# First row block of the attention scores as one full-precision product, another order of the turned sets

## Chip, cores and metric

One core of one Trainium2 chip. The time is that of one launch in device microseconds (us). The profile shows TensorE in two columns, PE (matmul) and PEld (weight load), beside DVE (VectorE), ACT (ScalarE), POOL (GpSimd) and SP (SyncE, which issues the DMAs).

## The reference, cut to what matters

Sixteen sequences of 512 tokens, width 128, 16 heads of 64: a modulated layer norm, causal attention, and a mixture of 8 experts with top 2. The change touches the attention alone.

```python
h = _layernorm(x) * (1 + ca) + sa
q, k, v = einsum('bsd,dhk->bshk', h, W_Q), ... W_K, ... W_V
scores = einsum('bqhc,bshc->bhqs', q, k) / sqrt(64)
probs = softmax(where(triu(ones, k=1), -1e6, scores))
z = einsum('bhqs,bshc->bqhc', probs, v)
x = x + ga * (einsum('bqhc,chd->bqd', z, W_out) + b_out)
h = _layernorm(x) * (1 + cb) + sb
x = x + gb * moe(h)
```

## The kernel before

First the attention of all 16 sequences (some 1150 us), then the experts of all. In the attention the unit of work is a pair of heads: `b` is the sequence, `p` the pair (8 in each, 128 in all), and `body` of TensorE runs once for each pair. Products that need more than the rounded fp32r format are made of three: high by high, low by high, high by low, where the low part is what rounding left (`split_product`, and the loop at L570 to L579 for scores). ScalarE rounds the high part (`round_q`, `round_k`), VectorE subtracts for the low part (`rest_q`, `rest_k`).

The causal score matrix of one head has four row blocks of 128 queries: row r has (r + 1) x 128 keys. `UNITS` groups them: unit 0 is row 3 (PSUM banks 2 and 3, one for each head), unit 1 is rows 2 and 0 (banks 4 and 5), unit 2 is row 1 (banks 6 and 7). The two heads lie in the two halves of the partitions, so a score product takes 64 rows of the array.

In order, TensorE's iteration for pair p (L716 to L793): scores of p, units 0, 1, 2; the product of probabilities and values for pair p-2 (`weigh_values`, full fp32, one half of the array's columns for each head); projections q and k of pair p+1; for some p one or more value chunks (`V_CHUNKS`), for p = 2 and 6 a part of the output projection; then the transposes of the probabilities of p-1 in three sets. Set 0 is 8 blocks of head 0, set 1 is 8 blocks of head 1, set 2 is 4 blocks of both. A block is turned in two halves (16, 16 and 8 transposes). Their order before is 2, 0, 1: set 2 to banks 4 and 5, set 0 to banks 6 and 7, set 1 to banks 0 and 1 (`T_PAIR`).

The other engines, for each pair: VectorE masks the scores and takes the row maxima (`mask_and_max`, L1239; in the order of units, head 0 then head 1), computes `rest_z`, `rest_q`, `rest_k`, and copies sets 2 and 0 out of PSUM (`evac_T`, L1232, 512 and 1024 elements for each partition), each after its transposes are counted in `t_ps`. ScalarE computes the exponentials with their sums (`exponentials`, L954), rounds z, q and k, copies a value chunk, and copies set 1 (`evac_T`, L945). GpSimd multiplies the eight row parts by the inverse sums (L501), as VectorE's `invert_sums` (L1248) has given them; it counts them in `p_norm`.

Banks tie the engines together. Scores of unit 1 go where VectorE's first copy of the iteration before has read, those of unit 2 where its second copy has: L569 waits for `t_dve` at 2(8b+p) - 3 and - 2, two counts a pair.

```python
if not young and u > 0:
    pe.wait_ge(t_dve, pair(2, b, p) - (3, 2)[u - 1])
```

The transposes wait for the masks that read their banks (`s_masked`) and for all eight norms of their pair (`p_norm`). `batches_from_middle` only places the loop's seam; each engine's order is the one written.

Of the kernel before, what the change touches and what calls it, by code (L numbers as in the profile page):

```python
# [20 lines left out]
UNITS = [[3], [2, 0], [1]]  # L21
ROW_AT = {3: 0, 2: 512, 0: 896, 1: 1024}
ROW_IN_BANK = {3: 0, 2: 0, 0: 384, 1: 0}
# [21 lines left out]
def masked_at(h, u):  # L45

    return (h, 2 + 2 * h, 6 + h)[u]
# [10 lines left out]
def adaln_moe_kernel(nc, resid, W_Q, W_K, W_V, W_out, b_out, W1, b1, W2, b2, Wr, br, c_in, wmod, out):  # L58
# [10 lines left out]
    with ExitStack() as ctx:  # L69
# [13 lines left out]
        T_PAIR, T_PAIR_END = [6, 0, 4], [0, 4, 6]  # L83
        T_PLACE = [2, 3, 1]
# [68 lines left out]
        side = banks[:, 4:6, 256:512].rearrange("p a (t s) -> p t a s", s=DH)  # L153
# [45 lines left out]
        with ExitStack() as pb:  # L199
# [31 lines left out]
            rdenom = sa("rdenom", [P, 2, 8])  # L231

# [123 lines left out]
            q_lo = sem("q_lo")  # L356
            k_lo = sem("k_lo")
# [15 lines left out]
            with nc.Block() as block:  # L373
# [67 lines left out]
                def _(pool):  # L441
# [47 lines left out]
                    def body(b, first, last):  # L489
                        for p in range(NP):  # L490
# [6 lines left out]
                            for h in range(2):  # L497
                                for r in ROW_ORDER:
# [4 lines left out]
                                        .then_inc(p_norm, 1)  # L503

                    batches(pool, body)
# [14 lines left out]
                def _(pe):  # L520
# [38 lines left out]
                    def scores(b, p, u, begin, young):  # L559
# [4 lines left out]
                        if young and not begin:  # L564

                            pe.wait_ge(s_masked, (2, 6, 8)[u])
# [3 lines left out]
                        for r in UNITS[u]:  # L570
                            n = (r + 1) * P
# [37 lines left out]
                    def values(b, p, n, i):  # L609
# [5 lines left out]
                        pe.wait_ge(s_masked, pair(8, b, p) + (7, 2)[n])  # L615
# [100 lines left out]
                    def body(b, first, last):  # L716
                        for p in range(NP):
# [14 lines left out]
                            scores(b, p, 0, begin, young)  # L732
                            if p == 5 and last:
                                pe.wait_ge(x_mid, b)
                            if p == 6 and last:
                                pe.wait_ge(r_full, 1)
                            scores(b, p, 1, begin, young)
# [34 lines left out]
                            if not begin:  # L772
                                pe.wait_ge(s_masked, done + 6)
# [6 lines left out]
                                if 0 in put:  # L780
                                    pe.wait_ge(v_done, 8 * b + now[len(put) - 1 - put[::-1].index(0)] + 1)
                                if p == 6 and not last:
                                    pe.wait_ge(h_full, b + 2)
                                    if not first:
                                        pe.wait_ge(x_mid, b)
                                wait_alone(pe, s_masked, done + 8)
                                transposes(*prev, 0, T_PAIR[0])
# [58 lines left out]
                    wait_alone(pe, p_norm, pair(8, end, NP))  # L846
                    transposes(end, NP - 1, 2, T_PAIR_END[2])
                    wait_alone(pe, hid, 2)
# [71 lines left out]
                def _(act):  # L920
# [187 lines left out]
                    def rear(b, p, first, last):  # L1108
# [16 lines left out]
                        if begin:  # L1125
                            round_weights(3)
# [466 lines left out]
```

## Time and profile before

| | us |
|---|---|
| runs of the kernel before, median of 3 (lowest, highest) | 1879.13 (1876.46, 1879.55) |
| the profiled execution, its own time | 1881.74 |
| its span, first to last instruction | 1879.9 |
| PE busy in it | 1865.9 |
| DVE / ACT / POOL busy | 1642.9 / 1558.2 / 729.7 |
| mean granted TensorE clock | 0.998 |

Busy time overlaps between engines. A matmul's duration in the profile holds its way through the array, so that consecutive ones overlap: what one costs is the distance from its start to the next one's start. "x2" in a row of the timeline is a group of two instructions; here mostly the two heads, which start together.

### The profile page before, as it was taken

What the parts mean: (1) busy time and instruction counts of PE and PEld (TensorE: products, weight loads), DVE (VectorE), ACT (ScalarE), POOL (GpSimd) and SP (SyncE); (2) the same over time, 40 slices, a digit from 0 to 9 for tenths busy, and PEclk for the clock granted to TensorE, in tenths of its full rate; (3) what the DMA queues carried; (4) which work ended last, traced back from release to release, by engine and by line L of the source; (5) the groups of instructions that cost most, each with busy time, mean ns of one, the idle gap of its engine ahead of it and who ended that gap; (6) DMA issues with size and microseconds to landing.
All of it is one profiled execution on the core that took longest, in us unless ns stands there. A gap on an engine that the chain in (4) does not pass through costs nothing.

```text
span 1879.9 us, 50582 instructions
## 1 busy us (share of the span) xinstructions
PE 1865.9 (99%) x15334; PEld 1431.6 (76%) x15334; DVE 1642.9 (87%) x4388; ACT 1558.2 (83%) x3664; POOL 729.7 (39%) x1212
## 2 busy tenths in 40 slices
PE   8999999999999999999999999999999999999999
PEld 6777777777777777777777777888888888888887
DVE  7898888888888888888888888989998999999998
ACT  6988988988998998998988988777777777777775
POOL 3454454454454444544445442222222222222221
PEclk9999999999999999999999999999999999999999
DMA  4200000000000000000000003111111111111111
GB/s 122 69 2 1 1 1 1 1 1 1 1 1 0 1 1 0 1 1 0 1 1 1 1 2 91 52 51 51 51 51 51 51 51 51 51 51 51 51 56 51
DMA packets 42622, 50.04 MB, mean 27 GB/s; under 512 B 3160, under 2 KB 24464, under 8 KB 42512
## 3 DMA queue, kind: packets, MB, share of 16 engines
q1 hardware_dynamic: 42256, 48.41, 8.1%
q0 software_dynamic: 256, 0.53, 0.1%
q14 instruction: 86, 0.70, 0.1%
q8 instruction: 24, 0.39, 0.1%
HBM read 44.47 MB, written 4.46 MB: 26 GB/s over the span
## 4 chain that ended last, share of the span: by engine, by line
PE 97%; DVE 1%; ACT 1%; issue 1%; DMA 0%; SPq 0%; ACTq 0%; DVEq 0%
PE banks L605 16%; PE banks L578 13%; PE banks L592 9%; PE banks L684 6%; PE banks L686 6%; PE banks L685 6%; PE banks L703 6%; PE banks L705 6%; PE banks L704 6%; PE banks L523 6%; PE banks L525 5%; PE banks L524 5%; PE banks L627 2%; PE banks L629 2%; PE banks L628 2%
## 5 line engine op out<-in xcount | busy, mean ns | idle before, releaser
L501 POOL TENSOR_SCALAR probs<-probs,rdenom 128x512 f32<-128x512 f32 (+3 forms) x1024 | 523.9, 533 | 584.5 <-DVE rdenom L1248 584.5
L954 ACT ACTIVATE probs<-probs,neg_max 128x512 f32<-128x512 f32 (+3 forms) x1024 | 561.8, 551 | 52.0 <-DVE neg_max L1239 52.0
L1059 ACT ACTIVATE hidden<-banks,b_cols 128x512 f32<-128x512 f32 x512 | 349.5, 688 | 177.7 <-PE banks L686 177.4
L1418 DVE TENSOR_TENSOR hid_lo<-hidden,hid_hi 128x512 fp32r<-128x512 f32 x512 | 380.3, 754 | 56.8 <-ACT hid_hi L1067 42.0
L1239 DVE CUSTOM_DVE_ANT_0 probs<-banks,mask_w 128x512 f32<-128x512 f32 (+3 forms) x1024 | 427.1, 482 | 0.7 <-PE banks L578 0.7
L487 POOL TENSOR_TENSOR acc<-acc,y_w 128x512 f32<-128x512 f32 x110 | 151.4, 1377 | 462.8 <-DVE y_w L1431 461.0
L605 PE MATMUL banks<-probs_T,v_sb 128*64 128x512 f32 (+3 forms) x2048 | 304.6, 440 | 0.3 <-issue 0.3
L1232 DVE COPY probs_T<-banks 128x512 f32<-128x512 f32 (+1 forms) x256 | 232.6, 949 | 30.0 <-PE banks L592 30.0
L605 PEld LDWEIGHTS banks<-probs_T,v_sb 128*64 128x64 f32 x2048 | 136.4, 137 | 155.7 <-issue 119.4
L592 PEld LDWEIGHTS banks<-ident,probs 64*128 64x128 f32 x5120 | 171.7, 140 | 45.3 <-issue 45.3
L684 PE MATMUL banks<-h_hi,w_hi 128*128 128x512 f32 x512 | 205.8, 402 | 0.1
L685 PE MATMUL banks<-h_hi,w_lo 128*128 128x512 f32 x512 | 199.6, 390 | 0.0
L686 PE MATMUL banks<-h_lo,w_hi 128*128 128x512 f32 x512 | 199.6, 390 | 0.0
L703 PE MATMUL banks<-hid_hi,w_hi 128*128 128x512 f32 x508 | 197.8, 389 | 0.0
L705 PE MATMUL banks<-hid_lo,w_hi 128*128 128x512 f32 x508 | 197.7, 389 | 0.0
L704 PE MATMUL banks<-hid_hi,w_lo 128*128 128x512 f32 x508 | 197.6, 389 | 0.0
L954 ACT ACTIVATION_READ_ACCUMULATOR probs<-probs,neg_max 128x1 f32 x1024 | 192.7, 188 | 0.0
L592 PE MATMUL banks<-ident,probs 64*128 64x64 f32 x5120 | 189.1, 226 | 0.7 <-ACT hidden L1059 0.6
L578 PE MATMUL banks<-k_hi,q_hi 64*128 64x512 f32 (+3 forms) x1024 | 177.6, 340 | 4.2 <-DVE probs_T L1232 2.1
L1252 DVE TENSOR_TENSOR z_lo<-banks,z_hi 128x512 fp32r<-128x512 f32 x128 | 88.3, 690 | 94.2 <-ACT z_hi L966 94.2
L578 PE MATMUL banks<-k_hi,q_lo 64*128 64x512 f32 (+3 forms) x1024 | 167.3, 320 | 0.0
L578 PE MATMUL banks<-k_lo,q_hi 64*128 64x512 f32 (+3 forms) x1024 | 166.5, 319 | 0.0
(182 smaller groups left out, 3393.3 us busy)
## 6 DMA issues: line engine op xcount, KB each, us to landing
w_rows<-w_kept SPq DMA_DIRECT2D x128, 256.0 KB, 4.5
x_all<-in_L_attn_resid_dram SPq DMA_DIRECT2D x16, 256.0 KB, 2.8
w_raw<-in_L_ffn_W_dram SPq DMA_DIRECT2D x16, 256.0 KB, 4.8
out_dram<-y_result SPq DMA_DIRECT2D x15, 256.0 KB, 2.3
v_sb<-in_L_attn_W_V_dram SPq DMA_DIRECT2D x1, 512.0 KB, 9.8
hidden<-in_L_attn_W_out_dram POOLq DMA_DIRECT2D x2, 256.0 KB, 7.7
v_sb<-in_L_attn_W_Q_dram SPq DMA_DIRECT2D x1, 448.0 KB, 6.3
v_sb<-in_L_attn_W_K_dram SPq DMA_DIRECT2D x1, 448.0 KB, 7.5
```

The costliest lines, as they stand in the source:

```text
L501: pool.tensor_scalar(part, part, rdenom[:, p % 2, 4 * h + r:4 * h + r + 1], 1.0, ALU.mult, ALU.mult)\
L578: mm = pe.matmul(S_BANK[u][h][:, at:at + n], q[own, p % 2, rows], k[own, p % 2, 0:n], start=start, stop=stop)
L592: mm = pe.transpose(banks[:, first_bank + half, at:at + DH], probs[own, p % 2, h, src:src + P], ident[own, own])
L605: mm = pe.matmul(bank[h * DH:(h + 1) * DH, c * P:S], v_sb[:, c, hc:hc + DH], probs_T[:, h, KEY_AT[c]:KEY_AT[c] + n], start=(c == 0), stop= ...
L684: pe.matmul(banks[:, c, :], w1_hi[:, e, cols], h_hi[:, :], start=True, stop=False)
L685: pe.matmul(banks[:, c, :], w1_lo[:, e, cols], h_hi[:, :], start=False, stop=False)
L686: pe.matmul(banks[:, c, :], w1_hi[:, e, cols], h_lo[:, :], start=False, stop=True)\
L703: pe.matmul(y_bank, w2_hi[:, e, c, :], hi, start=(c == 0), stop=False)
L954: act.activation(part, part, ACT.Exp, bias=neg_max[:, p % 2, col:col + 1], scale=-1.0, accum_out=denom[:, p % 2, col:col + 1]).then_inc(p_ ...
L1059: act.activation(hidden[:, e % 2, c, :], banks[:, c, :], ACT.Gelu, bias=b1_cols[:, e * HC + c:e * HC + c + 1]).then_inc(hid, 1)
L1239: dve.tensor_tensor_reduce(out=probs[:, p % 2, h, at:at + n], in0=S_BANK[u][h][:, col:col + n], in1=mask_w[:, 512 - n:512], scale=-SCALE, ...
L1418: dve.tensor_tensor(hid_lo[:, e % 2, c, :], full, hi.bitcast(F32), ALU.subtract)\
```

## The change

The row blocks are grouped anew: unit 1 is row 2 alone, unit 2 is rows 1 and 0 (banks 6 and 7). Row 0 (128 x 128) is no longer three fp32r products for each head, but one in full fp32, from `q_full` and `k_full`, the sums of high and low parts. GpSimd makes these sums in a new step `join`, two instructions a pair behind the norms, and TensorE waits for them (`q_whole`, `k_whole`) ahead of row 0.

The sets are turned in the order 0, 2, 1: set 0 to banks 4 and 5, set 2 to banks 6 and 7, set 1 to banks 0 and 1 as before. Set 0 waits for four norms and the masks of units 0 and 1, set 2 for all. The waits for value chunk, h and x that go with banks 6 and 7 come ahead of set 2. VectorE's copies follow: set 0 first, then set 2. `invert_sums` moves behind the two masks of unit 0. On ScalarE both value chunks stand ahead of the exponentials of head 0, unit 2, and the copy of set 1 stands ahead of the exponentials of head 1, unit 2.

```diff
 ROW_ORDER = [3, 2, 0, 1]
-UNITS = [[3], [2, 0], [1]]
+UNITS = [[3], [2], [1, 0]]
 ROW_AT = {3: 0, 2: 512, 0: 896, 1: 1024}
-ROW_IN_BANK = {3: 0, 2: 0, 0: 384, 1: 0}
+ROW_IN_BANK = {3: 0, 2: 0, 0: 256, 1: 0}
 HEAD_COLS = 1280
...
-    return (h, 2 + 2 * h, 6 + h)[u]
+    return (h, 2 + h, 4 + 2 * h)[u]
...
-        T_PAIR, T_PAIR_END = [6, 0, 4], [0, 4, 6]
-        T_PLACE = [2, 3, 1]
+        T_PAIR, T_PAIR_END = [4, 0, 6], [6, 4, 0]
+        T_PLACE = [1, 3, 2]
...
-        side = banks[:, 4:6, 256:512].rearrange("p a (t s) -> p t a s", s=DH)
+        side = banks[:, 6:8, 256:512].rearrange("p a (t s) -> p t a s", s=DH)
...
             rdenom = sa("rdenom", [P, 2, 8])
+            q_full = sa("q_full", [P, 2, P])
+            k_full = sa("k_full", [P, 2, P])
...
             q_lo = sem("q_lo")
+            q_whole, k_whole = sem("q_whole"), sem("k_whole")
             k_lo = sem("k_lo")
             t_dve = sem("t_dve")
             s_masked = sem("s_masked")
...
+                            if not (last and p >= NP - 2):
+                                join(*after(*after(b, p)))
...
+                    def join(b, p):
...
+                        wait_alone(pool, q_lo, pair(1, b, p) + 1)
+                        pool.tensor_tensor(q_full[:, p % 2, :], q_hi2[:, p % 2, 0:P].bitcast(F32),
+                                           q_lo2[:, p % 2, 0:P].bitcast(F32), ALU.add).then_inc(q_whole, 1)
+                        wait_alone(pool, k_lo, pair(1, b, p) + 1)
+                        pool.tensor_tensor(k_full[:, p % 2, :], k_hi2[:, p % 2, 0:P].bitcast(F32),
+                                           k_lo2[:, p % 2, 0:P].bitcast(F32), ALU.add).then_inc(k_whole, 1)
...
+                    join(0, 0)
+                    join(0, 1)
                     batches(pool, body)
...
-                            pe.wait_ge(s_masked, (2, 6, 8)[u])
+                            pe.wait_ge(s_masked, (2, 4, 8)[u])
                         if not young and u > 0:
...
                         for r in UNITS[u]:
+                            if r == 0:
+                                pe.wait_ge(q_whole, pair(1, b, p) + 1)
+                                pe.wait_ge(k_whole, pair(1, b, p) + 1)
+                                at = ROW_IN_BANK[0]
+                                for h in range(2):
+                                    own = slice(h * DH, (h + 1) * DH)
+                                    mm = pe.matmul(S_BANK[u][h][:, at:at + P], q_full[own, p % 2, :],
+                                                   k_full[own, p % 2, :], start=True, stop=True)
+                                continue
                             n = (r + 1) * P
                             at = ROW_IN_BANK[r]
                             rows = slice(r * P, (r + 1) * P)
...
-                        pe.wait_ge(s_masked, pair(8, b, p) + (7, 2)[n])
+                        pe.wait_ge(s_masked, pair(8, b, p) + (6, 2)[n])
                         toks, cols = slice(t * P, (t + 1) * P), slice(half * 512, half * 512 + 512)
                         split_product(V_BANK[n], (h_hi[:, toks], h_lo[:, toks]),
                                       (wv[0][:, cols], wv[1][:, cols])).then_inc(v_ps, 1)
...
                             scores(b, p, 0, begin, young)
+                            scores(b, p, 1, begin, young)
                             if p == 5 and last:
                                 pe.wait_ge(x_mid, b)
                             if p == 6 and last:
                                 pe.wait_ge(r_full, 1)
-                            scores(b, p, 1, begin, young)
                             if begin:
                                 pe.wait_ge(b_ok, 1)
                             scores(b, p, 2, begin, young)
...
                             if not begin:
-                                pe.wait_ge(s_masked, done + 6)
+                                pe.wait_ge(s_masked, done + 4)
+                                wait_alone(pe, p_norm, pair(8, *prev) + 4)
+                                transposes(*prev, 0, T_PAIR[0])
+                                if 0 in put:
+                                    pe.wait_ge(v_done, 8 * b + now[len(put) - 1 - put[::-1].index(0)] + 1)
+                                if p == 6 and not last:
+                                    pe.wait_ge(h_full, b + 2)
+                                    if not first:
+                                        pe.wait_ge(x_mid, b)
+                                pe.wait_ge(s_masked, done + 8)
                                 if p == 4 and last:
                                     attention_T_beside(b - 1)
                                 if p == 5 and last:
                                     norm_T_beside(0)
                                 wait_alone(pe, p_norm, pair(8, *prev) + 8)
                                 transposes(*prev, 2, T_PAIR[2])
-                                if 0 in put:
-                                    pe.wait_ge(v_done, 8 * b + now[len(put) - 1 - put[::-1].index(0)] + 1)
-                                if p == 6 and not last:
-                                    pe.wait_ge(h_full, b + 2)
-                                    if not first:
-                                        pe.wait_ge(x_mid, b)
-                                wait_alone(pe, s_masked, done + 8)
-                                transposes(*prev, 0, T_PAIR[0])
                                 if not young:
                                     pe.wait_ge(z_done, pair(1, *prev))
                                 if has_next:
...
                     wait_alone(pe, p_norm, pair(8, end, NP))
+                    transposes(end, NP - 1, 0, T_PAIR_END[0])
+                    wait_alone(pe, hid, 2)
                     transposes(end, NP - 1, 2, T_PAIR_END[2])
-                    wait_alone(pe, hid, 2)
-                    transposes(end, NP - 1, 0, T_PAIR_END[0])
                     wait_alone(pe, z_done, pair(1, end, NP - 1))
                     transposes(end, NP - 1, 1, T_PAIR_END[1])
                     pe.wait_ge(o_half, B)
...
                         exponentials(b, p, 0, 1)
-                        exponentials(b, p, 1, 1, [2])
+                        exponentials(b, p, 1, 1)
                         if not (first and p < 2):
                             round_z(*two_before(b, p))
                         if has_next and not begin:
...
                         put = chunk_banks(p, first, last)
-                        if now:
-                            values_out(b, put[0], now[0])
-                        exponentials(b, p, 1, 1, [0])
-                        if len(now) > 1:
-                            values_out(b, put[1], now[1])
+                        for bank, i in zip(put[:2], now[:2]):
+                            values_out(b, bank, i)
                         exponentials(b, p, 0, 2)
...
                             values_out(b, n, i)
-                        exponentials(b, p, 1, 2)
+                        if begin:
+                            exponentials(b, p, 1, 2)
                         if p == 5 and last:
-                            act.wait_ge(t_dve, pair(2, *prev) + 1)
+                            act.wait_ge(t_dve, pair(2, *prev) + 2)
                             router_h_evac(0, in_halves(hf[:, :]), side)
                         if p == 6 and not last:
                             half_out(b)
...
                             evac_T(*prev, first and p == 1)
+                            exponentials(b, p, 1, 2)
                         if begin:
                             round_weights(3)
...
                         begin, nxt = first and p == 0, after(b, p)
+                        mask_and_max(b, p, 0, 0)
+                        mask_and_max(b, p, 1, 0)
                         if not begin:
                             invert_sums(*before(b, p))
-                        mask_and_max(b, p, 0, 0)
-                        mask_and_max(b, p, 1, 0)
                         mask_and_max(b, p, 0, 1)
                         if begin:
                             rest_q(*nxt)
...
                         if not begin:
+                            evac_T(*prev, 0, first and p == 1, T_PAIR[0])
                             evac_T(*prev, 2, first and p == 1, T_PAIR[2])
                         if p == 4 and last:
                             add_attention(b - 1)
-                        if not begin:
-                            evac_T(*prev, 0, first and p == 1, T_PAIR[0])
...
                     split_expert(1, 3)
+                    evac_T(end, NP - 1, 0, False, T_PAIR_END[0])
                     evac_T(end, NP - 1, 2, False, T_PAIR_END[2])
-                    evac_T(end, NP - 1, 0, False, T_PAIR_END[0])
                     weights(0)
                     for e in range(4, E):
                         split_expert(1, e)
...
```

## Rows read from the trace of the kernel before

**Rows 1.** The page: busy time of each engine, and the chain that ended last.

```profile
PE 1865.9 (99%) x15334; PEld 1431.6 (76%) x15334; DVE 1642.9 (87%) x4388; ACT 1558.2 (83%) x3664; POOL 729.7 (39%) x1212
...
PE 97%; DVE 1%; ACT 1%; issue 1%; DMA 0%; SPq 0%; ACTq 0%; DVEq 0%
```

**Rows 2.** Timeline, PE, two iterations' transposes; start us, us, engine, line, operation.

```profile
407.61 1.48 PE L592 MATMUL banks<-ident,probs 64*128 64x64 f32 x40
...
415.57 1.47 PE L592 MATMUL banks<-ident,probs 64*128 64x64 f32 x40
```

**Rows 3.** Timeline, PE, the scores of the pair between them.

```profile
408.90 0.48 PE L578 MATMUL banks<-k_hi,q_hi 64*128 64x512 f32 x2
...
410.21 0.22 PE L578 MATMUL banks<-k_hi,q_hi 64*128 64x128 f32 x2
...
410.38 0.28 PE L578 MATMUL banks<-k_lo,q_hi 64*128 64x128 f32 x2
410.49 0.34 PE L578 MATMUL banks<-k_hi,q_hi 64*128 64x256 f32 x2
...
410.78 0.28 PE L578 MATMUL banks<-k_lo,q_hi 64*128 64x256 f32 x2
410.99 0.65 PE L605 MATMUL banks<-probs_T,v_sb 128*64 128x512 f32 x2
```

**Rows 4.** Timeline, PE, full fp32: first and last key block of one product with values.

```profile
403.04 1.08 PE L605 MATMUL banks<-probs_T,v_sb 128*64 128x512 f32 x4
...
405.02 0.39 PE L605 MATMUL banks<-probs_T,v_sb 128*64 128x128 f32 x4
```

**Rows 5.** Timeline, DVE, its copies beside the transposes at 407.61.

```profile
407.67 0.69 DVE L1225 TENSOR_TENSOR k_lo<-banks,k_hi 128x512 fp32r<-128x512 f32 x1
408.27 1.81 DVE L1232 COPY probs_T<-banks 128x512 f32<-128x512 f32 x2
410.00 0.19 DVE L1248 RECIPROCAL rdenom<-denom 128x8 f32<-128x8 f32 x1
```

**Rows 6.** Timeline, PE and DVE, a copy that waited for its transposes.

```profile
189.69 0.79 PE L592 MATMUL banks<-ident,probs 64*128 64x64 f32 x18
...
190.20 0.69 DVE L1232 COPY probs_T<-banks 128x512 f32<-128x512 f32 x1 [0.23 <-PE banks L592]
```

**Rows 7.** Timeline, DVE and PE, scores of row 1 that waited for a copy.

```profile
1108.80 1.21 DVE L1232 COPY probs_T<-banks 128x1024 f32<-128x1024 f32 x1
1109.93 0.19 DVE L1248 RECIPROCAL rdenom<-denom 128x8 f32<-128x8 f32 x1
...
1110.07 0.39 PE L578 MATMUL banks<-k_hi,q_hi 64*128 64x256 f32 x2
1110.29 0.28 PE L578 MATMUL banks<-k_hi,q_lo 64*128 64x256 f32 x2
...
1110.62 0.65 PE L605 MATMUL banks<-probs_T,v_sb 128*64 128x512 f32 x2
```

**Rows 8.** Timeline, DVE and PE, the iteration with p = 2.

```profile
181.05 1.47 PE L592 MATMUL banks<-ident,probs 64*128 64x64 f32 x40
...
181.28 0.75 DVE L1262 SCALAR_TENSOR_TENSOR attn_T<-banks,gate_cols,o_part 128x512 f32<-128x512 f32 x1 [1.53 <-PE banks L629]
181.95 1.81 DVE L1232 COPY probs_T<-banks 128x512 f32<-128x512 f32 x2
...
184.43 1.94 PE L605 MATMUL banks<-probs_T,v_sb 128*64 128x512 f32 x10
```

**Rows 9.** Timeline, ACT, its copy of set 1 and the exponentials after it.

```profile
409.58 1.00 ACT L945 ACTIVATE probs_T<-banks 128x1024 f32<-128x1024 f32 x1
410.79 0.72 ACT L954 ACTIVATE probs<-probs,neg_max 128x512 f32<-128x512 f32 x1 [0.20 <-DVE neg_max L1239]
```

**Rows 10.** Timeline, POOL: eight norms; and the page's group of its sums of two tensors.

```profile
410.36 4.09 POOL L501 TENSOR_SCALAR probs<-probs,rdenom 128x512 f32<-128x512 f32 x8 [3.98 <-DVE rdenom L1248]
...
L487 POOL TENSOR_TENSOR acc<-acc,y_w 128x512 f32<-128x512 f32 x110 | 151.4, 1377 | 462.8 <-DVE y_w L1431 461.0
```

## The prediction

> **What bounds the kernel now.** The page comes first: PE is busy 1865.9 of 1879.9 us, and the chain that ended last is PE for 97% [rows 1]. So every microsecond taken off TensorE's own stream counts, unless another engine hands its data over later than the shortened stream wants it. How much each hand-over has in reserve isn't in the page. I read it from the timeline of ordinary pairs, where nobody is shown to wait: from the start T of one pair's transposes to the next is 7.96 us [rows 2]. All times below are counted from T = 407.61. Scores begin at T + 1.29, row 0 at T + 2.60, row 1 at T + 2.88, the product with values at T + 3.38 [rows 3]. From there to the next T are 415.57 - 410.99 = 4.58 us that the change leaves as they are. The other half of the iteration belongs to VectorE, whose two copies run from T + 0.66 to T + 2.47 [rows 5]. Unit 1 of the next scores needs the first of them, unit 2 the second.
>
> **What TensorE's stream saves.** Row 0 takes 410.49 - 410.21 = 0.28 us a pair [rows 3], 36 us in 128 pairs. Its later steps are 0.11 us apart though 128 columns pass in half of that (the 256-column steps aren't longer): weight loads set the pace, and they go on setting it in row 1. The new product: one of full fp32 is two instructions for each head. Four of 128 columns span 0.39 us of which 0.28 is the last pair's duration, so the two heads go side by side and a step costs 0.11 us [rows 4]. For row 0 that makes 2 x 0.11 = 0.22. These rows split the array by columns; the scores split it by rows, and no row here shows full fp32 in that form. Bounds: 0.22 (two steps, as there) to 0.44 (four in a row). I take 0.22, because in every split form in the rows (transposes, scores, values) the heads start together as "x2".
> Without any wait: row 1 would start at T + 2.60 (its weights load under row 2), its three steps 0.12 + 0.12 + 0.11, row 0 0.22, then the 0.10 that the switch to the other split costs (410.99 - 410.78 = 0.21, less the 0.11 of a 256-column pass) [rows 3]. That is T + 3.27 for the product with values, 0.11 earlier than now: 14 us in 126 pairs, 0.8%.
>
> **What the new order of copies takes.** Now the 512-element copy of set 2 goes first. It needs only 8 transposes and VectorE is free later than that, so the copies run right behind `rest_k`, at T + 0.66 [rows 5]. In the new order the first copy needs the 16 transposes of set 0. Twenty starts in 1.47 us, the last 0.22 long and the first gap 0.12, give 0.063 us for a pair of transposes [rows 2], so the eighth pair starts at T + 0.49. A copy that waits starts 0.26 to 0.27 us behind its last transposes (190.20 against 189.69 + 0.12 + 2 x 0.063) [rows 6]: T + 0.76. The 1024-element copy hands over after 1.13 us (1109.93 - 1108.80) [rows 7], the 512-element one lasts 0.68 (1.81 less 1.13) [rows 5]. The second copy ends at T + 0.76 + 1.13 + 0.68 = T + 2.57 to 2.58, which is 0.1 later than today. But unit 2 is wanted 0.28 earlier, since row 0 has left the place ahead of it: at T + 2.60, and its weights sooner. Today's reserve of 0.40 us (T + 2.88 against 2.47) shrinks to 0.02.
> What too little reserve costs is seen where scores of row 1 wait: the copy ends at 1110.01, the product is shown at 1110.07 and the next step comes 0.22 later instead of 0.17, and from the first to the product with values it is 0.55 instead of 0.50, as the first weights load in the open [rows 3, 7]. For the new unit 2 this gives 0.055 from the copy, then 0.22 + 0.12 + 0.11 for row 1, 0.22 for row 0 and 0.10 for the switch: T + 2.575 + 0.055 + 0.775 = T + 3.41. Today it is T + 3.38. **The pair gets 0.03 us longer**, though TensorE has 0.11 us less to do. Unit 1's wait (first copy ends at T + 1.97, its first product is wanted at T + 2.07) loses up to 0.08 us, hidden by the later wait of unit 2.
> **The pair after p = 2** is worse. There `gate_attention` holds the copies until T + 0.90 (181.95 against 181.05) in either order. The second ends at 181.95 + 1.13 + 0.68 = 183.76, the product with values starts at 184.59, today at 184.43 [rows 8]: 0.16 us longer, 15 times.
>
> **The other edits**, each with what hides it.
> GpSimd's two sums a pair: a norm of 128 elements is a part of 4.09 us for eight, a sum of two tensors of 512 takes 1.38 us [rows 10], so 0.3 to 1.4 us for each; I take 0.55. The queue holds norms for 4.1 of 7.96 us, and the sums come behind them, ahead of the next norms. Their inputs are ready by T + 0.8 (`rest_k` ends at 408.36 [rows 5]), their reader is row 0 of the next scores, at T + 2.95. Cost 0; at 1.4 each they would be done at T + 3.3 and hold row 0 up by 0.3.
> `invert_sums` behind two masks: VectorE's sum is the same, the norms start 1.2 to 1.3 us later, at T + 4.0 (410.36 - 407.61 + 1.25 [rows 2, 10]) and end at T + 8.1, which is 0.15 into the next transposes. Set 0 asks for half of them and set 2 for all, at 0.55 into the transposes: 0.4 us of reserve. Cost 0.
> ScalarE: the copy of set 1 starts when its transposes are done, T + 1.52 (20 pairs and the 0.26), instead of T + 1.97 [rows 9]; head 1's last two exponentials (some 0.9 us) follow, and the next pair's first one starts at T + 3.3 instead of T + 3.18. It has one exponential fewer ahead of `round_z`, so z, q and k are rounded no later than now, and q and k wait for TensorE anyway. Nobody waits for ScalarE; cost 0. At the end of an iteration ScalarE is free about 0.05 us before set 1 is turned, so nothing is lost in waiting.
> The waits for value chunks, h and x move behind 16 transposes, to a later place; cost 0, gain 0, as PE shows no wait there. Start and end (the first two pairs, the last sets): within 1 us.
>
> **The sum.** 111 pairs x 0.03 + 15 x 0.16 = 3.3 + 2.4 = 5.7 us. The profiled execution gives 1881.74 + 5.7 = 1887.4 us. It lies 2.6 above the median of the runs, 1879.13, so for the median I forecast **1885 us**, 0.3% slower.
>
> **Rivals.**
> *The heads don't go side by side in row 0*, so the change doesn't do what it says. If the instructions started in strict program order (head 0 twice, then head 1 twice) row 0 would take three steps instead of two; behind the wait that is 0.11 us more in 128 pairs, 14 us: 1899 us. Against it: four 512-column instructions with values span 1.08 us, of which 0.6 is the last pair, so four start within two steps [rows 4]. Wholly in a row: 28 us, 1913.
> The Trainium skill ("TensorE: Matmul & The Clock Gate", Part 3, The mechanism) says matmuls are in program order in start and end, "strict FIFO, no reordering". By that rule this rival holds; the rows with values don't agree with it, and none shows the split by rows.
> *The copies don't bind*: if the second copy came 0.1 us sooner than I make it (a sooner start, or weights that load ahead of the wait), the whole 0.11 us would stay: 14 us, 1865 us. For it: my reserve of 0.02 us is the difference of long sums. Against: a copy has never started less than 0.26 behind its transposes in the rows, and half of the gain needs 0.09.
> *The norms come late*: if GpSimd's norms and sums end over 0.4 us later than I reckon, set 2 waits at every pair. At 0.1 us a pair that is 13 us: 1898 us.
>
> **Chances.** Forecast with its own spread (a pair from -0.02 to +0.07 us, 1877 to 1889): 0.60. Heads one after another 0.17, of which 1899 0.13. Copies don't bind 0.13, half of that gain 0.06. Norms late 0.04. Range: 1868 to 1901 us, which leaves out the full gain and the worst of the first rival. A measurement of this kernel can tell 0.2% from no change (1875.4 to 1882.9). Within the forecast most lies above that: slower 0.40, same 0.18, faster 0.02. With the rivals: slower 0.61, same 0.20, faster 0.19.
>
> **What the profile after would show.** Row 0 as four full fp32 instructions, two steps of 0.11 us, where the first rival has three or four. VectorE's copies in the order 1024, 512, each time with a wait of about 0.1 us for transposes ahead of the first. A line in the waits that PEld at the scores waits for VectorE's copy, over a hundred times. A distance from transposes to transposes of 7.98 to 8.00 us in ordinary pairs; 7.85 would prove the second rival. POOL busy some 140 us more. I am wrong if the scores' waits aren't there, or if the ordinary pair is shorter than 7.94.

## The result, and the profile after

The changed kernel takes 1886.5 us (median of 5 runs, 1885.94 to 1887.52), the kernel before beside it 1879.5 us: ratio 1.0038, 95% interval 1.0027 to 1.0050. It is 0.4% slower; 1885 us was forecast. The profiled execution of the changed kernel took 1886.59 us, 4.9 more than that of the kernel before.

From the page after: span, busy time, the chain that ended last.

```profile
span 1884.7 us, 50756 instructions
...
PE 1867.5 (99%) x15078; PEld 1399.2 (74%) x15078; DVE 1660.1 (88%) x4388; ACT 1559.1 (83%) x3664; POOL 847.5 (45%) x1468
...
PE 96%; DVE 1%; ACT 1%; issue 1%; POOL 0%; DMA 0%; SPq 0%; ACTq 0%; DVEq 0%; POOLq 0%
```

The page hardly differs from that of before [rows 1]: 256 matmuls fewer and PE as busy as ever, since a matmul that waits for its weights is drawn as busy (the 384-column one below takes 0.41 us, before it took 0.33). The list of waits (engine and line, who was waited for, us in all, times, longest), before and after, says more:

```profile
PEld banks L578 <- DVE probs_T L1232: 3.9, 5, 1.9
```

```profile
PEld banks L603 <- DVE probs_T L1257: 35.5, 124, 1.6
```

TensorE's weights for scores (L603) now wait for a copy of VectorE (L1257) 124 times; before, such a wait was there 5 times. In an ordinary pair the wait that is listed is that of unit 1, for the first copy. Weight load (PEld) of the 384-column product:

```profile
409.98 0.19 PEld L603 LDWEIGHTS banks<-k_hi,q_hi 64*128 64x128 f32 x2 [0.25 <-DVE probs_T L1257]
```

Timeline of the changed kernel, PE, one ordinary pair (start us, us, engine, line):

```profile
407.94 1.47 PE L617 MATMUL banks<-ident,probs 64*128 64x64 f32 x40
...
410.01 0.41 PE L603 MATMUL banks<-k_hi,q_hi 64*128 64x384 f32 x2
410.26 0.34 PE L603 MATMUL banks<-k_hi,q_lo 64*128 64x384 f32 x2
...
410.61 0.35 PE L603 MATMUL banks<-k_hi,q_hi 64*128 64x256 f32 x2
410.80 0.28 PE L603 MATMUL banks<-k_hi,q_lo 64*128 64x256 f32 x2
...
411.04 0.38 PE L593 MATMUL banks<-k_full,q_full 64*128 64x128 f32 x4
411.35 0.65 PE L630 MATMUL banks<-probs_T,v_sb 128*64 128x512 f32 x2
```

And DVE in the same pair:

```profile
407.98 0.69 DVE L1250 TENSOR_TENSOR k_lo<-banks,k_hi 128x512 fp32r<-128x512 f32 x1
408.70 1.82 DVE L1257 COPY probs_T<-banks 128x1024 f32<-128x1024 f32 x2
```

With T = 407.94 the first copy starts at T + 0.76 and the second ends at T + 2.58 (408.70 + 1.82). Unit 1 starts at T + 2.07, as before, but its first step is 0.25 instead of 0.17. Unit 2 is shown to start at T + 2.67, its first step is 0.19 instead of the 0.12 of a hidden weight load, and the product with values starts at T + 3.41. It was T + 3.38 [rows 3]. Row 0 itself went as hoped: four instructions in 0.38 us, 0.31 from its start to the next product, switch included. After p = 2 the gated attention holds the copies, as before [rows 8]; PE and DVE of the changed kernel:

```profile
391.16 1.48 PE L617 MATMUL banks<-ident,probs 64*128 64x64 f32 x40
...
392.05 1.81 DVE L1257 COPY probs_T<-banks 128x1024 f32<-128x1024 f32 x2
...
394.69 0.65 PE L630 MATMUL banks<-probs_T,v_sb 128*64 128x512 f32 x2
```

That is T + 3.53, forecast 3.54. Seven pairs in a row, from the transposes after p = 2 on, in the kernel before and then in the changed one:

```profile
391.02 1.47 PE L592 MATMUL banks<-ident,probs 64*128 64x64 f32 x40
...
451.00 1.47 PE L592 MATMUL banks<-ident,probs 64*128 64x64 f32 x40
```

```profile
391.16 1.48 PE L617 MATMUL banks<-ident,probs 64*128 64x64 f32 x40
...
451.49 1.47 PE L617 MATMUL banks<-ident,probs 64*128 64x64 f32 x40
```

59.98 us became 60.33: 0.35 more, where the working gave 0.16 + 6 x 0.03 = 0.34. The eighth pair brings it to some 0.39 a sequence, or 6 us in 126 pairs. The two profiled executions differ by a little less. A possible reason is seen in the stretch 0 to 36 us and the stretch 1090 to 1160 us (busy time of each engine, then the granted clock of TensorE), before and after:

```profile
0.00:36.00 36.00, 29.70 (x199) 24.07 (x201) 23.18 (x76) 22.74 (x54) 10.99 (x26) 0.95 0.46 129
1090.00:1160.00 70.00, 67.23 (x651) 48.44 (x650) 58.30 (x156) 57.88 (x140) 25.51 (x48) 0.98 0.18 55
```

```profile
0.00:36.00 36.00, 29.43 (x208) 22.91 (x208) 25.89 (x86) 24.43 (x60) 14.27 (x34) 1.00 0.45 132
1090.00:1160.00 70.00, 65.51 (x641) 46.05 (x638) 58.76 (x167) 57.39 (x146) 35.14 (x67) 1.00 0.11 30
```

The granted clock of the execution before was 0.95 and 0.98 in the mean of these stretches, so it was at the lower of its two levels (1.2 and 2.4 GHz) for a part of them; in the execution after it was 1.00. These are single executions, so I ascribe no microseconds of the median to it.

### The profile page after: what moved, and what is told of

Same layout as the page of the kernel before. It is cut to its first block, busy times and chain, and to the rows that moved or that the text cites. A ratio compares the mean times of both kernels' runs of the same rounds, so it can differ in the third digit from the quotient of the medians.

```text
span 1884.7 us, 50756 instructions
## 1 busy us (share of the span) xinstructions
PE 1867.5 (99%) x15078; PEld 1399.2 (74%) x15078; DVE 1660.1 (88%) x4388; ACT 1559.1 (83%) x3664; POOL 847.5 (45%) x1468
## 4 chain that ended last, share of the span: by engine, by line
PE 96%; DVE 1%; ACT 1%; issue 1%; POOL 0%; DMA 0%; SPq 0%; ACTq 0%; DVEq 0%; POOLq 0%
PE banks L630 15%; PE banks L603 12%; PE banks L617 9%; PE banks L709 6%; PE banks L710 6%; PE banks L711 6%; PE banks L728 6%; PE banks L730 6%; PE banks L729 6%; PE banks L539 6%; PE banks L541 5%; PE banks L540 4%; PE banks L652 2%; PE banks L654 2%; PE banks L653 2%; PE banks L593 1%
## 5 line engine op out<-in xcount | busy, mean ns | idle before, releaser
L1264 DVE CUSTOM_DVE_ANT_0 probs<-banks,mask_w 128x512 f32<-128x512 f32 (+3 forms) x1024 | 433.5, 479 | 0.5 <-PE banks L603 0.4
L1257 DVE COPY probs_T<-banks 128x1024 f32<-128x1024 f32 (+1 forms) x256 | 233.0, 952 | 39.5 <-PE banks L617 38.2
L971 ACT ACTIVATE probs_T<-banks 128x1024 f32<-128x1024 f32 x128 | 131.3, 1026 | 52.7 <-PE banks L617 52.6
L603 PE MATMUL banks<-k_hi,q_hi 64*128 64x512 f32 (+2 forms) x768 | 159.9, 412 | 5.4 <-DVE probs_T L1257 3.2
L1093 ACT ACTIVATE hid_hi<-hidden 128x512 fp32r<-128x512 f32 x256 | 161.1, 629 | 0.0
```

Source lines behind the costliest of these rows:

```text
L603: mm = pe.matmul(S_BANK[u][h][:, at:at + n], q[own, p % 2, rows], k[own, p % 2, 0:n], start=start, stop=stop)
L1264: dve.tensor_tensor_reduce(out=probs[:, p % 2, h, at:at + n], in0=S_BANK[u][h][:, col:col + n], in1=mask_w[:, 512 - n:512], scale=-SCALE, ...
```

## Experiments

All ratios are to the kernel before, run on the same chip; times in a pair are counted from the start of its transposes, T.

### The product alone

```diff
 UNITS = [[3], [2, 0], [1]]
...
                         for r in UNITS[u]:
+                            if r == 0:
+                                pe.wait_ge(q_whole, pair(1, b, p) + 1)
+                                pe.wait_ge(k_whole, pair(1, b, p) + 1)
+                                ...
```

(and `join` on GpSimd, as in the change; nothing else.)

> The kernel before with one part of the change alone: row 0 as one full fp32 product with GpSimd's sums; units, order of the sets, VectorE and ScalarE as before. My theory (the product saves 0.11 us a pair of TensorE's time and VectorE's second copy took it away): unit 2 is wanted at T + 2.82, the second copy ends at T + 2.47, so nothing waits; product with values 0.11 us earlier in each pair, 14 us less, ratio to the kernel before 0.9925. Rival A (the product saves nothing on TensorE, or the sums on GpSimd slow another engine): ratio 1.000 or above. Rival B (three small products cost less than the start distances say): half the gain, 0.996.

Measured: 1867.26 us, ratio 0.9939 (0.9926 to 0.9953). PE and DVE in an ordinary pair:

```profile
410.76 1.47 PE L617 MATMUL banks<-ident,probs 64*128 64x64 f32 x40
...
413.35 0.38 PE L593 MATMUL banks<-k_full,q_full 64*128 64x128 f32 x4
413.49 0.36 PE L603 MATMUL banks<-k_hi,q_hi 64*128 64x256 f32 x2
...
414.02 0.65 PE L630 MATMUL banks<-probs_T,v_sb 128*64 128x512 f32 x2
```

```profile
411.57 1.81 DVE L1257 COPY probs_T<-banks 128x512 f32<-128x512 f32 x2
```

The product with values starts at T + 3.26, 0.12 earlier than before. The second copy ends at T + 2.62 (411.57 + 1.81 - 410.76) and row 1, which needs it, is shown at T + 2.73: the reserve is down to 0.1 us and still enough. The saving in TensorE's time was priced rightly for an ordinary pair, and no cost of the sums shows there. In the run it is a little less: 11 us between the medians (interval 9 to 14), where 14 were expected. The timelines of the two profiled executions do differ by some 0.88 us a sequence, 14 us in 16; why the medians differ by less stays open. This version is faster than the kernel before by 0.6% and, with both ratios to that kernel, than the changed one by 1.0%.

### The second copy made shorter

The changed kernel, where VectorE's copy of set 2 takes head 0's part only; head 1's part of these blocks keeps the first pair's values.

```diff
-                        dve.tensor_copy(*turned(u, first_bank)).then_inc(t_dve, 1)
+                        out, turned_p = turned(u, first_bank)
+                        if u == 2 and not begin:
+                            out, turned_p = out[:, 0], turned_p[:, 0]
+                        dve.tensor_copy(out, turned_p).then_inc(t_dve, 1)
```

> The changed kernel, but VectorE's copy of set 2 takes head 0's half alone (256 elements of 512; head 1's part of these blocks keeps what the first pair left), all else as changed. My theory: the second copy ends 0.27 us sooner, T + 2.30, and no longer holds unit 2; only unit 1's wait for the first copy is left (0 to 0.08 us): product with values at T + 3.27 to 3.33, ratio to the kernel before 0.994 to 0.997. If the wait for the second copy were not what ate the gain, the ratio would stay at 1.004.

Measured: 1877.08 us, ratio 0.9988 (0.9979 to 0.9998). PE and DVE:

```profile
404.51 1.47 PE L617 MATMUL banks<-ident,probs 64*128 64x64 f32 x40
...
406.58 0.42 PE L603 MATMUL banks<-k_hi,q_hi 64*128 64x384 f32 x2
406.83 0.34 PE L603 MATMUL banks<-k_hi,q_lo 64*128 64x384 f32 x2
...
407.18 0.29 PE L603 MATMUL banks<-k_hi,q_hi 64*128 64x256 f32 x2
...
407.86 0.65 PE L630 MATMUL banks<-probs_T,v_sb 128*64 128x512 f32 x2
```

```profile
405.27 1.56 DVE L1260 COPY probs_T<-banks 128x1024 f32<-128x1024 f32 x2
```

The copies end 0.26 us sooner, and unit 2 takes 0.12 for its first step again: its weight load starts 0.18 us ahead of the product (at 407.00), in the changed kernel 0.04 (at 410.57). The product with values starts at T + 3.35 instead of 3.41. But unit 2 still starts at T + 2.67, and the listed wait of the weights is unchanged:

```profile
PEld banks L603 <- DVE probs_T L1260: 35.5, 124, 1.6
```

That wait is unit 1's: its first step is 0.25 instead of 0.17, with the first copy ending at T + 1.98, less than a weight load (0.19) ahead of T + 2.07. So of the 0.15 us between T + 3.26 and T + 3.41 the second copy accounts for 0.06 and the first for the 0.08 or so that are left. The expectation was missed by a little: the ratio lies above the 0.994 to 0.997 (its interval too), and T + 3.35 above the 3.27 to 3.33.

### Row 0 as three products in the changed order

```diff
                         for r in UNITS[u]:
-                            if r == 0:
-                                ...
-                                continue
```

(`join` is left out too.)

> The changed kernel with row 0 as three fp32r products again (as the last of unit 2) and no sums on GpSimd; all orders as in the changed kernel. My theory: behind the wait for the copy each pair has 0.22 + 0.12 + 0.12 + 0.11 + 0.11 + about 0.2 us to the product with values, T + 3.50, 0.12 us more than before in ordinary pairs: 17 us more, ratio 1.009. If the copy's wait did not set the pace it would be 1.000, and if GpSimd's sums were what costs in the changed kernel it would be under 1.004.

Measured: 1893.03 us, ratio 1.0079 (1.0064 to 1.0095). PE:

```profile
409.52 1.47 PE L594 MATMUL banks<-ident,probs 64*128 64x64 f32 x40
...
412.18 0.35 PE L580 MATMUL banks<-k_hi,q_hi 64*128 64x256 f32 x2
...
412.98 0.65 PE L607 MATMUL banks<-probs_T,v_sb 128*64 128x512 f32 x2
```

Unit 2 is shown to start at T + 2.66, as in the changed kernel (2.67), and the product with values at T + 3.46. The start is the same whatever is multiplied behind it. That the second copy sets it isn't shown: it is T + 2.67 with the shorter copy too, since unit 1 comes 0.08 us late. What the full product saves behind the start is 0.05 us in the timeline, not the 0.09 that I had taken, and 6.5 us between the medians. The three small products cost less than I took: in this timeline the first of row 0 is followed by the next after 0.06 us.

### The inverse sums late, alone

```diff
-                        if not begin:
-                            invert_sums(*before(b, p))
                         mask_and_max(b, p, 0, 0)
                         mask_and_max(b, p, 1, 0)
+                        if not begin:
+                            invert_sums(*before(b, p))
```

> The kernel before with the inverse sums moved behind the two masks of unit 0, nothing else. My theory: the norms end at T + 8.1 us, and set 2, first of the sets here, waits for all eight. In the four pairs of a sequence whose transposes come 7.95 us after the last ones TensorE waits 0.2 to 0.3 us, in the others (8.6 us and more) it does not: 64 x 0.27 = 17 us more, ratio 1.009. If GpSimd has more reserve than I read, the ratio is 1.000.

Measured: 1891.43 us, ratio 1.0071 (1.0056 to 1.0087). Transposes start 8.15 us apart in the short pairs (409.39 and 417.54) where it was 7.96, as they stand behind GpSimd's norms:

```profile
409.39 1.48 PE L592 MATMUL banks<-ident,probs 64*128 64x64 f32 x40
417.54 1.48 PE L592 MATMUL banks<-ident,probs 64*128 64x64 f32 x40
```

```profile
405.21 4.08 POOL L501 TENSOR_SCALAR probs<-probs,rdenom 128x512 f32<-128x512 f32 x8 [4.32 <-DVE rdenom L1248]
```

The norms end at 409.29, the transposes start 0.10 later. So the late sums do cost where the set that is turned first asks for all eight norms; in the changed kernel it asks for four.

### The old order of the sets

The changed kernel with T_PAIR, the transposes and VectorE's copies in the order 2, 0, 1 again, and the sums early again:

```diff
-        T_PAIR, T_PAIR_END = [4, 0, 6], [6, 4, 0]
-        T_PLACE = [1, 3, 2]
+        T_PAIR, T_PAIR_END = [6, 0, 4], [0, 4, 6]
+        T_PLACE = [2, 3, 1]
...
+                        if not begin:
+                            invert_sums(*before(b, p))
                         mask_and_max(b, p, 0, 0)
                         mask_and_max(b, p, 1, 0)
-                        if not begin:
-                            invert_sums(*before(b, p))
```

> The changed kernel with the sets turned and copied in the order of before (2, 0, 1) and the inverse sums again ahead of the masks; row 0 in full fp32 as the last of unit 2, and ScalarE's new order, stay. My theory: the second copy ends at T + 2.47 and unit 2 is wanted at T + 2.60, a reserve of 0.13 us, just enough; the full 0.11 us a pair shows: ratio to the kernel before 0.9925. If ScalarE's order or the sums on GpSimd made the changed kernel slow, it stays at 1.000 to 1.004.

Measured: 1926.2 us, ratio 1.0254 (1.0240 to 1.0268): far off what I expected. DVE:

```profile
404.12 1.81 DVE L1256 COPY probs_T<-banks 128x512 f32<-128x512 f32 x2
406.76 0.20 DVE L1272 RECIPROCAL rdenom<-denom 128x8 f32<-128x8 f32 x1 [0.83 <-ACT probs L979]
```

The reciprocal of the sums waits 0.83 us for ScalarE (99.3 us in 124 pairs). ScalarE's new order puts two exponentials behind its copy of set 1; with the sums early, VectorE's masks stand behind these. I had treated the moves of the sums and of ScalarE's copy as two free edits; the late sums turn out to be what makes ScalarE's order bearable. The same kernel with the sums late takes 1890.43 us, with ScalarE's old order 1891.22 us (both below).

### ScalarE's order alone

In the kernel before:

```diff
-                        exponentials(b, p, 1, 1, [2])
+                        exponentials(b, p, 1, 1)
...
-                        if now:
-                            values_out(b, put[0], now[0])
-                        exponentials(b, p, 1, 1, [0])
-                        if len(now) > 1:
-                            values_out(b, put[1], now[1])
+                        for bank, i in zip(put[:2], now[:2]):
+                            values_out(b, bank, i)
...
-                        exponentials(b, p, 1, 2)
+                        if begin:
+                            exponentials(b, p, 1, 2)
...
                             evac_T(*prev, first and p == 1)
+                            exponentials(b, p, 1, 2)
```

> The kernel before with ScalarE's new order alone: both value chunks ahead of the last exponentials of head 0, the copy of set 1 ahead of those of head 1. After the run with the old sets my theory is: the inverse sums stand ahead of the masks here and need all eight exponentials; ScalarE ends the last at T + 3.3 us instead of T + 2.3, so VectorE stops for 0.9 us in each pair and the masks, copies and scores behind it come late: ratio 1.010 to 1.030, with a wait of DVE for ACT at the reciprocal in over a hundred pairs. Rival (what made the run with the old sets slow was the place of row 0 or the small reserve of unit 2): ratio 1.000, no such wait.

Measured: 1952.82 us, ratio 1.0394 (1.0378 to 1.0410). The sign is as the theory has it, the size is more, and the wait is shorter and rarer than I said:

```profile
DVE rdenom L1247 <- ACT probs L954: 44.0, 62, 1.1
```

So the wait at the reciprocal isn't all. With row 0 still in unit 1, this order also has one exponential more ahead of `round_z`. How the rest of the 73 us divides was not taken apart.

### The old sets with ScalarE's old order

The kernel with the old order of the sets, with ScalarE's order of before as well (the copy of set 1 behind all exponentials); of the change the full product as last of unit 2 stays.

```diff
-                        if begin:
-                            exponentials(b, p, 1, 2)
+                        exponentials(b, p, 1, 2)
...
                             evac_T(*prev, first and p == 1)
-                            exponentials(b, p, 1, 2)
```

> The changed kernel with the sets, the inverse sums and ScalarE's order all as before; what stays of the change is the full product as the last of unit 2 and its sums. Theory of the order (ScalarE's late exponentials against early inverse sums): no stop at the reciprocal, unit 2 wanted at T + 2.60 against a second copy ending at T + 2.47, product with values at T + 3.27: ratio 0.994, as with the product alone. Rival (the reserve of 0.13 us is too small or row 0 in unit 2 costs): ratio above 0.997.

Measured: 1891.22 us, ratio 1.0063 (1.0049 to 1.0077). Neither theory names what it shows. ACT and PE:

```profile
411.36 1.01 ACT L970 ACTIVATE probs_T<-banks 128x1024 f32<-128x1024 f32 x1
```

```profile
412.00 0.38 PE L593 MATMUL banks<-k_full,q_full 64*128 64x128 f32 x4
412.46 1.08 PE L630 MATMUL banks<-probs_T,v_sb 128*64 128x512 f32 x4
```

From row 0 to the product with values it is 0.46 instead of 0.31: that product reads the copy of set 1, which ends at 412.37. With row 0 in unit 2 both of its exponentials stand between the rounding of k and this copy; before, head 0's stood ahead of `round_z`. The copy starts at T + 2.36 instead of T + 1.97 [rows 9]. That is what "ScalarE's copy ahead" is for.

### The old sets, the sums late

The kernel with the old order of the sets, with the sums late as in the change:

```diff
-                        if not begin:
-                            invert_sums(*before(b, p))
                         mask_and_max(b, p, 0, 0)
                         mask_and_max(b, p, 1, 0)
+                        if not begin:
+                            invert_sums(*before(b, p))
```

> The changed kernel with the sets turned and copied in the order of before (2, 0, 1); the late inverse sums and ScalarE's new order stay, so VectorE has nothing to stop for. My theory: unit 2 isn't held (copy ends at T + 2.47, wanted at T + 2.60), the copy of set 1 is in time, so the product with values comes at T + 3.27 in every pair; but set 2, turned first, waits for all eight norms, as with the late sums alone, where the short pairs took 8.15 us. Four pairs of eight take about 8.15 instead of 7.95, the other four 0.11 less than before: (4 x 0.2 - 4 x 0.11) x 16 = 6 us more, ratio 1.003. If the waits for norms are gone with the short stream, 0.994.

Measured: 1890.43 us, ratio 1.0058 (1.0042 to 1.0075); expected 1.003. PE and POOL:

```profile
409.52 1.43 PE L617 MATMUL banks<-ident,probs 64*128 64x64 f32 x39 [0.26 <-issue]
...
412.77 2.38 PE L630 MATMUL banks<-probs_T,v_sb 128*64 128x512 f32 x16
```

```profile
405.33 4.08 POOL L504 TENSOR_SCALAR probs<-probs,rdenom 128x512 f32<-128x512 f32 x8 [3.31 <-DVE rdenom L1272]
```

The product with values comes at T + 3.25, so no copy holds it in ordinary pairs, but the transposes wait: norms end at 409.41, transposes start at 409.52. After p = 2 the second copy holds unit 2 here too (the product with values comes at T + 3.52, before at 3.38), which I had left out; these pairs make up most of the difference between 1.003 and 1.0058. In both orders that were run with late sums, this one and the changed one, one of the two waits is paid.

### Row 0 back in unit 1, all else changed

```diff
-UNITS = [[3], [2], [1, 0]]
+UNITS = [[3], [2, 0], [1]]
-ROW_IN_BANK = {3: 0, 2: 0, 0: 256, 1: 0}
+ROW_IN_BANK = {3: 0, 2: 0, 0: 384, 1: 0}
...
-                                pe.wait_ge(s_masked, done + 4)
+                                pe.wait_ge(s_masked, done + 6)
```

> The changed kernel with row 0 back in unit 1, still one full fp32 product; the new order of sets, inverse sums and ScalarE stays. Unit 2 is then wanted at T + 2.82 against a second copy that ends at T + 2.58, so it does not wait; unit 1 waits for the first copy (end T + 1.97, first product 0.055 later, first step 0.28 instead of 0.17): product with values at T + 3.32, 0.06 us less than the kernel before, ratio 0.997; 1.004 if the wait lay elsewhere, 0.994 if unit 1's wait costs nothing.

Measured: 1899.39 us, ratio 1.0110 (1.0094 to 1.0125): I was wrong. In some pairs the product with values comes at T + 3.33, as I had it (3.32), in others at T + 3.65 to 3.69. The former show what the first copy costs by itself: unit 2 has no wait there, unit 1's first step is 0.25, and the product comes 0.07 us behind the T + 3.26 of the product alone. PE and DVE in one of those:

```profile
412.79 1.47 PE L617 MATMUL banks<-ident,probs 64*128 64x64 f32 x40
```

```profile
412.07 0.69 DVE L1277 TENSOR_TENSOR z_lo<-banks,z_hi 128x512 fp32r<-128x512 f32 x1 [0.32 <-ACT z_hi L992]
...
413.88 1.81 DVE L1257 COPY probs_T<-banks 128x1024 f32<-128x1024 f32 x2
```

The copies start at T + 1.09 instead of 0.76, held by `rest_z` and with it by ScalarE, which has six exponentials of an iteration ahead of `round_z` here (four in the changed kernel, five in the kernel before). The chain from ScalarE's roundings to VectorE's copies is the next one behind the transposes. In the changed kernel it is some 0.1 us away, an estimate: `rest_k` starts at T + 0.04 (407.98), and where nothing holds it the next instruction follows after 0.60 (413.28 to 413.88 here). I had left this chain out.

## Why the prediction was right, point by point

- **What binds.** The premise (TensorE's stream, and hand-overs read one by one from its timeline) held. A wait of the scores' weights for VectorE's copy is there 124 times, as forecast, and ordinary pairs are 7.97 to 8.00 us apart. But the listed wait is the one for the first copy, and it stays when the second is made shorter (35.5 us, 124 times in both kernels).
- **TensorE's saving.** 0.11 us a pair forecast, 0.12 measured with the product alone. Row 0's two heads go side by side: four instructions in 0.38 us, which with the 0.28 of a last pair [rows 4] is two steps of some 0.1. The rival that they do not (1899 us) falls.
  The rule of the Trainium skill ("TensorE: Matmul & The Clock Gate", Part 3, The mechanism) that matmuls start and end in strict program order would have given three steps and 1899 us; these rows don't agree with it, for the split by rows as for the split by columns [rows 4]. This takes the four instructions in the order in which the kernel asks for them, head 0 and then head 1; the profile doesn't show their order in the program.
- **The copies.** They start at T + 0.76 and end at T + 2.58, and the product with values comes at T + 3.41: as worked out, to 0.01 us. After p = 2: 3.53 against 3.54. The second rival (copies don't bind, 1865 us) falls; 0.12 us a pair was saved and 0.15 paid.
  The way to T + 3.41 was not as worked out. The prediction puts the whole loss down to the second copy and has unit 1's 0.08 us hidden behind it. The shorter second copy gives back only 0.06 and leaves unit 2's start at T + 2.67, and row 0 in unit 1 shows some 0.07 for the first copy alone. So unit 1's delay isn't hidden: by itself it brings unit 2 to T + 2.67, and the second copy adds to that only the longer first step. What the second copy would cost with the first in time was not run.
  Two terms are off in opposite directions as well. Unit 2 starts 0.09 behind the copy's end, not 0.055, and its first step is 0.19, not 0.22. (The five terms behind the start add up to 0.77, not 0.775.) That the time came out to 0.01 us is in part luck.
- **GpSimd's sums.** 0.46 us each, 0.55 taken. POOL is busy 118 us more, where I said some 140. The norms (changed kernel, POOL) end at 416.11, T + 8.17, or 0.17 into the next transposes, against 0.15 forecast, and set 2 asks for all of them at 0.55. The rival of late norms falls, with some 0.4 us to spare, but only thanks to the order of the sets: with set 2 first, norms as late cost 0.7% (the late sums alone; the old sets with late sums lost 0.6%).

```profile
408.21 0.46 POOL L513 TENSOR_TENSOR q_full<-q_hi,q_lo 128x128 f32<-128x128 f32 x1
...
412.03 4.08 POOL L504 TENSOR_SCALAR probs<-probs,rdenom 128x512 f32<-128x512 f32 x8 [2.75 <-DVE rdenom L1273]
```

- **ScalarE.** Copy at T + 1.52 and next exponential at T + 3.31, both as forecast:

```profile
409.46 1.03 ACT L971 ACTIVATE probs_T<-banks 128x1024 f32<-128x1024 f32 x1
...
411.25 0.71 ACT L980 ACTIVATE probs<-probs,neg_max 128x512 f32<-128x512 f32 x1
```

  Cost 0 was right for the change as a whole. What the prediction did not say, and the runs show, is that each of these edits is only free in company: the reciprocal behind the masks covers the late exponentials, the half wait for norms covers the late reciprocal, and the copy ahead of the exponentials covers row 0's place. Taken singly, the reciprocal cost 0.7% and ScalarE's order 3.9%, of which the wait at the reciprocal is only a part.
- **The sum.** 5.7 us forecast. The median moved by 7.0 (interval 5 to 9), the pairs in the timeline account for about 6. The rest lies within the interval of the measurement, and what of it is real stays open.

The gain of the new product (0.12 us a pair) is thus spent, and 0.03 more, by what its place in unit 2 drags along: the copy of set 1 has to go first, so the exponentials go last, so the sums come late, so the norms do, so the large set is turned first, so VectorE's copies start 0.1 us later. The first one is then too late for unit 1 by some 0.08 us, and the second costs unit 2, which is wanted 0.28 us earlier, another 0.06. Left in unit 1 with the old orders, row 0 needs none of it.

## What to carry to other kernels

When an engine's stream is full, read for each hand-over how long the data lies ready before it is wanted, and subtract every shortening and every reordering from that reserve; what a gain takes beyond the smallest reserve is lost again. Where several hand-overs follow each other in one stream, find out for each listed wait which of them it is, since a list by line puts them together. Try the cheap arithmetic edit alone, in its old place, before the reorderings that seem to go with it. And test a bundle of moves both ways: an edit that costs nothing in the bundle can cost 4% alone, so its price has to be stated with the edits that cover it.

## What was not expected of the hardware

- A hand-over costs more than its wait when weights load behind it: a first product of 384 columns takes 0.25 us to the next instead of 0.17 with the data only just in time (410.01 to 410.26 in the changed kernel), although it starts no later than before. Its weight load starts at 409.98, 0.03 us ahead of it; in the kernel with the product alone it starts 0.23 us ahead (412.60 against 412.83).
- A full fp32 product fits between two fp32r ones with nothing lost. In the kernel with the product alone, row 0 and the first step of row 1 take 0.34 us together (413.35 to 413.69), which is 0.22 + 0.12: no more than the two cost apart.
